# Latent attention: own query tiles summed by GpSimd, four absorbed weight tiles in place of six, and a new order around the shifts

## The chip, the cores and the metric

One core of a Trainium2 chip runs the whole kernel, one launch. The metric is the device time of that launch in microseconds (us), lower is better. The kernel before took 834.43 us (median of three runs, 832.11 to 836.56).

## The reference

The kernel computes a two-layer decoder on 4 x 256 tokens of 256 features. Only the layer-0 cross attention (latent attention with rotary positions) is touched here. Cut to what matters:

```python
q_hk  = (hidden_q @ Wq.T).reshape(B, S, H, K)          # H = 16 heads, K = 128
q_big = einsum('bshk,hkq->bshq', q_hk, w_kc_q)         # 192 latent features per head
q_big = q_big * cos + rotate_half(q_big) * sin         # halves of 96 features change places
kv_r  = kv_c * cos_k + rotate_half(kv_c) * sin_k       # 64 features, shared by all heads
q_r   = einsum('bshq,hqr->bhsr', q_big, W_qr)          # R = 64
k_r   = einsum('bld,hdr->bhlr', kv_r, W_kr)
p     = softmax(einsum('bhsr,bhlr->bhsl', q_r, k_r))
# the values are projected with w_kc_kv and Wo and added to x
```

## The kernel before, in words

`mla_stage` works on eight **pairs** of heads (`PAIRS = 8`), p = 0 to 7. There is no planner: each engine has its own program, written out by hand in queue order, and engines meet only in semaphores, so an instruction that waits holds up everything behind it on its engine. 1024 token columns are handled in two halves of 512 (one PSUM bank each).

Per pair, the query weights of both heads are **folded** (`fold`, L1474: `wq2` x `wkq`, 2 x 192 latent columns side by side). ScalarE copies the high part, VectorE writes the rest (`fold_rest`, L1216). The 384 latent columns make three tiles of 128: tile 0 belongs to head 0, tile 2 to head 1 (the **own** tiles), tile 1 holds 64 columns of each head (the **shared** tile). `packed(p, k)` (L1518, six one-pass matmuls each) projects one tile of one half into a PSUM bank, k = 0 to 5 in the order shared, own 0, own 2 for half 0, then half 1.

`rotate(p, k)` (VectorE) multiplies each bank by the cosine and by the sine table `tab` and writes both products to `qcs`: four 64-row instructions for the shared tile (L1201), two 128-row instructions for an own tile (L1208). The rotary swap of halves isn't done on the queries. Instead the absorbed weights exist twice: `turn` transposes `W_qr` and the key weight, `turned_weights` (ScalarE, L1359 to L1368) lays out six tiles in `wrT`, a plain and a swapped order, `absorb` (L1496) makes six 64-column products with `wkrT`, and `absorbed_weights` (VectorE, L1221) copies them (384 columns). A tile's cosine product meets the plain weights and its sine product the swapped ones, both accumulated in PSUM: `scored_shared` (L1532, two matmuls) and `scored_own` (L1539, four matmuls, each two passes).

The resulting queries leave PSUM as a high part (`query_high`, ScalarE, L1378, two 64-row copies per half) and a rest (`query_rest`, VectorE, L1226). `scores(p, k)`, k = 0 to 7 (L1557), gives scores of one sequence and head. `maximum` (VectorE, L1233) and `denominators` (ScalarE, L1389, two exponentials with sums) follow, then per half `logarithms` (L1394), `shifts` (VectorE, L1239 to L1247), `shift_transpose` (PE, L1567), and `shift_rows` (ScalarE, L1398), which issues two 4 KB DMAs (L1401) that place the shifts as two extra rows of `q2`. `scores_t` (L1595, L1596) needs those rows. It gives transposed, shifted scores, `exponentials` (L1409) makes probabilities, `product` (L1612) the contexts, `context_high` and `context_rest` (L1415, L1256) split them, `project` (L1626) multiplies by the output weight and `add` (L1263) adds to x.

The PE order of one pair is:

```python
project(p-1,0) packed(p,2) turn(p+1) project(p-1,1) packed(p,3) scored_shared(p,0)
project(p-1,2) packed(p,4) output_weight(p) scored_own(p,0) project(p-1,3) packed(p,5)
fold(p+1) scored_shared(p,1) scores(p,0..3) scored_own(p,1) absorb(p+1)
shift_transpose(p,0) scores(p,4..7) scores_t(p,0..1) packed(p+1,0) packed(p+1,1)
shift_transpose(p,1) product(p,0..1) scores_t(p,2..3) product(p,2..3)
```

The VectorE order is: add 0, rotate 2, add 1, rotate 3, add 2, rotate 4, weight_rest, add 3, query_rest twice, rotate 5, fold_rest, maximum 0 to 3, shifts(0), query_rest twice, absorbed_weights, maximum 4 to 7, shifts(1), rotate(p+1, 0 and 1), context_rest 0 to 3. GpSimd has, once per pair and after the first two scores_t, nine instructions (L1185, L1187, L1189) that round the weights of the feed-forward layer. SP issues the weight loads of the next pairs and the copies of the queries to `q2` (L1132).

Of the kernel before, what the change touches and what calls it, by code (L numbers as in the profile page):

```python
# [1007 lines left out]
class PairWeights:  # L1008


    def __init__(self, c, st):
# [7 lines left out]
        self.tab = sb("tab", [P, 2, 3, SEQ])  # L1019
# [15 lines left out]
    def first(self, sp):  # L1035
        self.load_a(sp, 0)
        self.load_k(sp, 0)
        self.load_n(sp, 0)
        sp.dma_start(self.tab[:, :, :, :], self.io["rope_q"]).then_inc(self.tab_in.sem, 16)


def mla_stage(c):
    nc, io = c.nc, c.io
    with ExitStack() as st:
# [9 lines left out]
        wrT, wkrT = sb("wrT", [P, 6, P]), sb("wkrT", [P, 2 * CTX])  # L1054
        wr = sb("wr", [P, 2, 2, 3, R])
# [25 lines left out]
        zeroed, tern = c.counter("at_m5"), c.counter("at_m4")  # L1081
# [40 lines left out]
        def seq_cols(b):  # L1122
            return slice(b * SEQ, (b + 1) * SEQ)

        with nc.Block() as block:

            @block.sync
            def _(sp):
# [18 lines left out]
                for p in range(PAIRS):  # L1147
# [46 lines left out]
            def _(dve):  # L1194
                def rotate(p, k):
# [23 lines left out]
                def absorbed_weights(p, bank):  # L1219
                    dve.wait_ge(absorbed.sem, p + 1)  # L1220
                    dve.tensor_scalar(wr[:, p % 2, :, :, :].rearrange("p j t n -> p (j t n)"),  # L1221
                                      c.ps[:, bank, 0:6 * R], 1.0, None, ALU.mult).then_inc(wr_done.sem, 1)
# [83 lines left out]
                dve.wait_ge(tab_in.sem, 16)  # L1306
# [5 lines left out]
                for p in range(PAIRS):  # L1312
# [37 lines left out]
            def _(act):  # L1350
# [4 lines left out]
                def turned_weights(p):  # L1355
# [3 lines left out]
                    act.activation(dst.rearrange("p (k n) -> p k n", n=DCQ)[:, 0:4:3, :],  # L1359
                                   ps[:, 0:2 * DCQ].rearrange("p (h n) -> p h n", h=2), ACT.Copy)\  # L1360
                        .then_inc(turned_ev.sem, 1)
                    act.activation(dst[:, DCQ:DCQ + 448].rearrange("p (h n) -> p h n", h=2)[:, :, 0:160],
                                   ps[:, 32:352].rearrange("p (h n) -> p h n", h=2), ACT.Copy).then_inc(turned_ev.sem, 1)
                    act.activation(dst[:, 352:416].rearrange("p (h n) -> p h n", h=2),
                                   ps[:, 0:2 * DCQ].rearrange("p (k n) -> p k n", n=32)[:, 0:12:11, :], ACT.Copy)\
                        .then_inc(turned_ev.sem, 1)
# [29 lines left out]
                def shift_rows(p, half):  # L1396
# [68 lines left out]
            def _(pe):  # L1465
                def fold(p):
# [22 lines left out]
                def absorb(p, bank):  # L1489
# [3 lines left out]
                    for j in range(2):  # L1493
                        for tile in range(3):
                            h = (0, j, 1)[tile]
                            mm = pe.matmul(c.ps[:, bank, (3 * j + tile) * R:(3 * j + tile + 1) * R],  # L1496
                                           wrT[:, WR_SLOTS[tile][j], :], wkrT[:, rows(h)],
                                           start=True, stop=True)
# [24 lines left out]
                def scored_shared(p, half):  # L1523
# [1715 lines left out]
```

## Time and profile before

| what | value |
|---|---|
| median of three runs | 834.43 us (832.11 to 836.56) |
| the profiled execution | 833.54 us, span 831.7 us |
| mean granted TensorE clock | 0.948 |
| this stage, from its first matmul to its last add | 113.7 to 425.3 us of the span |
| seven pairs (p = 1 to 7) | start 37.4 us apart |

The span runs from the first to the last instruction that the profile shows, and the run's own time holds 1.8 us around it. Times of single instructions below come from this one execution. PE is the matmul engine, DVE is VectorE, ACT ScalarE, POOL GpSimd, SP the queue that issues DMAs. An fp32 matmul shows as two PE instructions, one declared fp32r as one.

### The profile page before, as it was taken

What the parts mean: (1) busy time and instruction counts of PE and PEld (TensorE: products, weight loads), DVE (VectorE), ACT (ScalarE), POOL (GpSimd) and SP (SyncE); (2) the same over time, 40 slices, a digit from 0 to 9 for tenths busy, and PEclk for the clock granted to TensorE, in tenths of its full rate; (3) what the DMA queues carried; (4) which work ended last, traced back from release to release, by engine and by line L of the source; (5) the groups of instructions that cost most, each with busy time, mean ns of one, the idle gap of its engine ahead of it and who ended that gap; (6) DMA issues with size and microseconds to landing.
All of it is one profiled execution on the core that took longest, in us unless ns stands there. A gap on an engine that the chain in (4) does not pass through costs nothing. (4 is left out here: it accounts for less than half of the span.)

```text
span 831.7 us, 13300 instructions
## 1 busy us (share of the span) xinstructions
PE 720.5 (87%) x4814; PEld 462.6 (56%) x4826; DVE 576.9 (69%) x1109; ACT 430.5 (52%) x896; POOL 198.4 (24%) x298
## 2 busy tenths in 40 slices
PE   5999979999998989999847469999379999759998
PEld 3555656666665656666533345566234444348886
DVE  5678568676667657676569955565578999575666
ACT  4558734544636364543649655555256767433332
POOL 2413010303123030303135314220121111351350
PEclk9999999999999999999989779999869999958999
DMA  4624422120202111110144006220010333303111
GB/s 123 184 82 138 139 67 67 47 56 21 74 10 67 29 48 29 48 42 1 26 119 86 9 12 186 64 55 2 23 36 21 83 71 83 105 2 103 51 51 51
DMA packets 49760, 52.24 MB, mean 63 GB/s; under 512 B 10116, under 2 KB 40388, under 8 KB 49588
## 3 DMA queue, kind: packets, MB, share of 16 engines
q1 hardware_dynamic: 48982, 51.03, 22.6%
q8 instruction: 39, 0.64, 0.3%
q10 hardware_dynamic: 714, 0.37, 0.2%
q14 instruction: 25, 0.20, 0.1%
HBM read 26.58 MB, written 2.04 MB: 34 GB/s over the span
## 5 line engine op out<-in xcount | busy, mean ns | idle before, releaser
L427 DVE TENSOR_REDUCE a_nm<-ps 128x2 f32<-128x512 f32 (+1 forms) x112 | 75.4, 688 | 28.2 <-PE ps L723 18.1
L2480 DVE TENSOR_REDUCE x_nm<-ps 128x2 f32<-128x512 f32 x128 | 85.0, 687 | 13.0 <-PE ps L2621 10.8
L2565 ACT ACTIVATE x_pt<-ps 128x1024 f32<-128x1024 f32 x64 | 62.5, 1021 | 33.9 <-PE ps L2649 33.2
L1389 ACT ACTIVATE m_junk<-ps,m_nm 128x256 bf16<-128x256 f32 x128 | 58.7, 486 | 30.3 <-DVE m_nm L1233 30.3
L1518 PE MATMUL ps<-m_xp,m_mp 128*128 128x512 f32 x288 | 73.4, 395 | 1.0 <-DVE m_wr L1221 1.0
L1185 POOL TENSOR_SCALAR fw<-fw,finv 128x256 f32<-128x256 f32 x24 | 11.6, 485 | 232.8 <-PE ps L1596 232.8
L2621 PE MATMUL ps<-kx,a_qs 96*128 96x256 bf16 x256 | 52.3, 291 | 8.5 <-DMA a_qs<-a_ks 6.5
L1518 PEld LDWEIGHTS ps<-m_xp,m_mp 128*128 128x128 f32 x288 | 51.3, 188 | 13.1 <-issue 3.2
L3049 PE MATMUL ps<-x_xp,x_wp 128*128 128x512 f32 x216 | 55.1, 406 | 0.0
L1201 DVE TENSOR_TENSOR m_qcs<-ps,mw_tab 64x512 f32<-64x512 f32 x64 | 44.1, 689 | 7.6 <-PE ps L1518 4.3
L3049 PEld LDWEIGHTS ps<-x_xp,x_wp 128*128 128x128 f32 x216 | 41.2, 196 | 8.5
L1208 DVE TENSOR_TENSOR m_qcs<-ps,mw_tab 128x512 f32<-128x512 f32 x64 | 41.2, 685 | 5.4 <-PE ps L1518 4.9
L2665 PE MATMUL ps<-x_pt,a_ks 128*32 128x256 f32 x512 | 42.0, 400 | 2.6 <-DVE x_av L2489 2.6
L2621 PEld LDWEIGHTS ps<-kx,a_qs 96*128 96x128 bf16 x256 | 20.2, 101 | 41.9 <-issue 13.1
L1233 DVE TENSOR_REDUCE m_nm<-ps 128x2 f32<-128x512 f32 x64 | 40.2, 682 | 0.9 <-PE ps L1557 0.7
L2649 PE MATMUL ps<-a_qs,kx 98*128 98x512 bf16 x128 | 39.4, 391 | 0.0
L1557 PE MATMUL ps<-m_kHH,m_qs 128*128 128x256 f32 x128 | 34.7, 306 | 4.4 <-DVE m_qs L1226 4.2
L1409 ACT ACTIVATE m_pt<-ps 128x1024 f32<-128x1024 f32 x32 | 31.1, 1019 | 13.8 <-PE ps L1596 13.8
L575 ACT ACTIVATE a_pt<-ps 128x1024 f32<-128x1024 f32 x32 | 32.1, 1020 | 10.4 <-PE ps L758 10.4
L575 ACT ACTIVATE fw<-ps 128x1024 f32<-128x1024 f32 (+1 forms) x32 | 25.8, 810 | 21.9 <-PE ps L774 15.1
L1256 DVE TENSOR_TENSOR m_cp<-ps,m_cp 128x256 fp32r<-128x256 f32 x32 | 12.8, 420 | 34.0 <-ACT m_cp L1415 34.0
L1595 PE MATMUL ps<-m_qs,m_kHH 128*128 128x512 f32 x64 | 27.6, 431 | 9.8 <-issue 9.5
(305 smaller groups left out, 1692.2 us busy)
## 6 DMA issues: line engine op xcount, KB each, us to landing
a_qs<-a_parts SPq DMA_DIRECT2D x48, 128.0 KB
a_ks<-a_parts SPq DMA_DIRECT2D x48, 128.0 KB
m_q<-m_qs SPq DMA_DIRECT2D x32, 128.0 KB
x_gb<-scr_g SPq DMA_DIRECT2D x8, 512.0 KB, 3.7
fw<-in_f_w SPq DMA_DIRECT2D x12, 256.0 KB
a_qs<-a_ks SPq DMA_DIRECT2D x48, 64.0 KB
mw_wq<-in_m_wq SPq DMA_DIRECT2D x8, 256.0 KB, 2.9
mw_wo<-in_m_wo SPq DMA_DIRECT2D x8, 256.0 KB, 2.8
```

Source lines behind the costliest of these rows:

```text
L427: dve.tensor_reduce(dst, src, AX.X, ALU.max, negate=True).then_inc(mx_done.sem, 1)
L575: act.activation(pt[:, n % 2, kt, 0:banks * BANK], c.ps[:, 2 + 2 * kt:2 + 2 * kt + banks, :].rearrange("p b n -> p (b n)"), ACT.Exp, scale ...
L1201: dve.tensor_tensor(qcs[rows((cs, 1 - cs)[h]), half, 1, h, :].rearrange("p (b q) -> p b q", q=SEQ), c.ps[rows(h), QB_BANKS[k], :].rearrang ...
L1208: dve.tensor_tensor(qcs[:, half, tile, cs, :].rearrange("p (b q) -> p b q", q=SEQ), c.ps[:, QB_BANKS[k], :].rearrange("p (b q) -> p b q", ...
L1233: dve.tensor_reduce(nm[:, k // 4, first:first + QT], c.ps[:, S_BANKS[k % 4], :].rearrange("p (t k) -> p t k", t=QT), AX.X, ALU.max, negate ...
L1389: act.activation(junk[:, n % 4, :], c.ps[:, S_BANKS[k % 4], qt * SEQ:(qt + 1) * SEQ], ACT.Exp, bias=nm[:, k // 4, one], accum_out=den[:, k ...
L1518: mm = pe.matmul(c.ps[:, QB_BANKS[k], :], mp[:, p % 2, w, dt, tile * P:(tile + 1) * P], xp[:, x, dt, half_cols(half)], start=((dt, w, x) = ...
L2480: dve.tensor_reduce(nm[:, n % ITEMS, QT * u:QT * u + QT], c.ps[:, u % 2, :].rearrange("p (t k) -> p t k", t=QT), AX.X, ALU.max, negate=Tru ...
L2565: act.activation(pt[:, n % 2, kt, :], c.ps[:, 2 + 2 * kt:4 + 2 * kt, :].rearrange("p b n -> p (b n)"), ACT.Exp, scale=SCALE).then_inc(exp_ ...
L2621: mm = pe.matmul(c.ps[:, u % 2, qt * SEQ:(qt + 1) * SEQ], queries(slice(0, S_ROWS), n, u).squeeze(1)[:, qt * P:(qt + 1) * P], kx[0:S_ROWS, ...
L2665: mm = pe.matmul(c.ps[rows(h), 6, 0:SEQ], vs[:, QT * b + kt, g, :], pt[:, n % 2, kt, h * SEQ:(h + 1) * SEQ], start=(kt == 0), stop=(kt == ...
L3049: mm = pe.matmul(up_bank(j, half), wp[:, b, w, at:at + EH], xp[:, x, dt, cols(half)], start=((dt, w, x) == terms[0]), stop=((dt, w, x) == ...
```

## The change

The latent columns of each head are placed in another order: the own tile of a head now holds the first 64 columns of each of its two rotary halves (0 to 63 and 96 to 159), the shared tile the other 32 of each half. With that the rotary partner of a row of an own tile is 64 rows away in the same tile. `rotate` writes the sine product of an own tile already swapped (two 64-row instructions) and the cosine product as before (one of 128 rows), and GpSimd adds the two in `qcs`. So own tiles need the plain weights only: four weight tiles in `wrT` and `wr`, two matmuls in `scored_own`. `fold` writes its columns in two pieces each. VectorE makes the high part of the first head's queries in the second half and its rest before `shifts(p, 0)`, and PE puts `scores(p, 4)` before `shift_transpose(p, 0)`. SP issues one of the two shift DMAs of the first half. `packed(p+1, 1)` moves behind `product(p, 1)`, `rotate(p+1, 1)` behind two `context_rest`. The table load becomes seven DMAs.

```diff
-        self.tab = sb("tab", [P, 2, 3, SEQ])
+        self.tab = sb("tab", [P, 2, 2, SEQ])
-        sp.dma_start(self.tab[:, :, :, :], self.io["rope_q"]).then_inc(self.tab_in.sem, 16)
+        for tile, (to, rows, source) in (...seven pieces...):
+            sp.dma_start(self.tab[to:to + rows, :, tile, :], self.io["rope_q"][first:first + rows, :, k, :])\
+                .then_inc(self.tab_in.sem, 16)
@@ sync, end of each pair
                     copy_queries(p, 1)
+                    sp.wait_ge(mt.sem, 2 * p + 1)
+                    send_shifts(sp, 0, 1)
@@ gpsimd
+                def own_tile(p, half, h):
+                    pool.wait_ge(rope.sem, rotated(p, 3 * half + 2 + h))
+                    turned_part = qcs[:, half, OWN_TILES[h], 1, :]
+                    plain = qcs[:, half, OWN_TILES[h], 0, :]
+                    pool.tensor_tensor(plain, plain, turned_part, ALU.add).then_inc(whole.sem, 1)
+
+                own_tile(0, 0, 0)
                 for p in range(PAIRS):
+                    own_tile(p, 0, 1)
+                    own_tile(p, 1, 0)
+                    own_tile(p, 1, 1)
+                    if p + 1 < PAIRS:
+                        own_tile(p + 1, 0, 0)
                     pool.wait_ge(stt.sem, 4 * p + 2)
@@ vector: rotate, own tile
-                    for cs in range(2):
+                    for part in range(2):
                         dve.tensor_tensor(
-                            qcs[:, half, tile, cs, :].rearrange("p (b q) -> p b q", q=SEQ),
-                            c.ps[:, QB_BANKS[k], :].rearrange("p (b q) -> p b q", q=SEQ),
-                            tab[:, cs, tile, :].unsqueeze(1).broadcast_to([P, 2, SEQ]), ALU.mult)\
+                            qcs[rows(1 - part), half, tile, 1, :].rearrange("p (b q) -> p b q", q=SEQ),
+                            c.ps[rows(part), QB_BANKS[k], :].rearrange("p (b q) -> p b q", q=SEQ),
+                            tab[rows(part), 1, 0, :].unsqueeze(1).broadcast_to([R, 2, SEQ]), ALU.mult)\
                             .then_inc(rope.sem, 1)
+                    dve.tensor_tensor(
+                        qcs[:, half, tile, 0, :].rearrange("p (b q) -> p b q", q=SEQ),
+                        c.ps[:, QB_BANKS[k], :].rearrange("p (b q) -> p b q", q=SEQ),
+                        tab[:, 0, 0, :].unsqueeze(1).broadcast_to([P, 2, SEQ]), ALU.mult)\
+                        .then_inc(rope.sem, 1)
@@ vector: absorbed_weights, and a new query_high
-                                      c.ps[:, bank, 0:6 * R], 1.0, None, ALU.mult).then_inc(wr_done.sem, 1)
+                                      c.ps[:, bank, 0:4 * R], 1.0, None, ALU.mult).then_inc(wr_done.sem, 1)
+                def query_high(p):
+                    dve.wait_ge(qr.sem, 2 * p + 2)
+                    dve.tensor_scalar(qs[rows(0), 0, half_cols(1)], c.ps[rows(0), 5, :], 1.0, None, ALU.mult)\
+                        .then_inc(q_hi.sem, 1)
@@ vector: order
                         maximum(p, k)
+                    query_high(p)
+                    query_rest(p, 1, 0)
                     shifts(p, 0)
-                    query_rest(p, 1, 0)
                     query_rest(p, 1, 1)
                         rotate(p + 1, 0)
+                    context_rest(p, 0)
+                    context_rest(p, 1)
+                    if p + 1 < PAIRS:
                         rotate(p + 1, 1)
-                    for b in range(BATCH):
-                        context_rest(p, b)
+                    context_rest(p, 2)
+                    context_rest(p, 3)
@@ scalar: turned_weights (three copies of 384, 320 and 64 columns become four of 256, 128, 64 and 64)
@@ scalar: query_high, shift_rows
-                    for h in range(2):
+                    if half:
+                        act.wait_ge(q_hi.sem, 4 * p + 3)
+                    for h in range(half, 2):
-                    for h in range(2):
-                        act.dma_start(...)
+                    send_shifts(act, half, 0)
+                    if half:
+                        send_shifts(act, half, 1)
@@ tensor: fold, absorb, scored_own
-                            mm = pe.matmul(c.ps[:, 6 + dt, h * DCQ:(h + 1) * DCQ], wq2[:, h, dt * P:(dt + 1) * P],
-                                           wkq[:, h, :], start=True, stop=True)
+                            by_half = wkq[:, h, :].rearrange("p (s n) -> p s n", s=2)
+                            own, shared = ((0, P), (P, DCQ)) if h == 0 else ((DCQ + R, 2 * DCQ), (DCQ, DCQ + R))
+                            for (a, b), part in ((own, by_half[:, :, 0:OWN]), (shared, by_half[:, :, OWN:])):
+                                mm = pe.matmul(c.ps[:, 6 + dt, a:b], wq2[:, h, dt * P:(dt + 1) * P], part,
+                                               start=True, stop=True)
-                    for j in range(2):
-                        for tile in range(3):
+                    for slot in range(4):
-                    pe.wait_ge(rope.sem, rotated(p, 3 * half + 3))
-                    for cs in range(2):
-                        for h, tile in ((0, 0), (1, 2)):
+                    pe.wait_ge(whole.sem, whole.at(4 * p + 2 * half + 2))
+                    for h in range(2):
@@ tensor: order
+                    scores(p, 4)
                     shift_transpose(p, 0)
-                    for k in range(4, 8):
+                    for k in range(5, 8):
                         packed(p + 1, 0)
-                        packed(p + 1, 1)
                     shift_transpose(p, 1)
                     product(p, 0)
                     product(p, 1)
+                        packed(p + 1, 1)
```

## Rows read from the trace of the kernel before

**Rows 1.** The page: span, busy time of each engine.

```profile
PE 720.5 (87%) x4814; PEld 462.6 (56%) x4826; DVE 576.9 (69%) x1109; ACT 430.5 (52%) x896; POOL 198.4 (24%) x298
```

**Rows 2.** Busy time by stretch: us, then each engine's, PEclk, DMA share, GB/s.

```profile
198.70:236.10 37.40, 34.61 (x196) 23.07 (x195) 25.31 (x45) 18.40 (x55) 7.21 (x9) 1.00 0.15 43
...
370.40:373.80 3.40, 3.21 (x15) 3.24 (x16) 2.96 (x6) 1.37 (x6) 0.00 (x0) 0.50 0.35 80
```

**Rows 3.** Timeline of PE, pair 3: start, us, what, idle before and releaser.

```profile
236.09 0.98 PE L1626 MATMUL ps<-m_wn,m_cp 128*128 128x256 f32 x6
...
244.99 1.89 PE L1539 MATMUL ps<-m_qcs,m_wr 128*64 128x512 f32 x8
...
249.01 1.46 PE L1474 MATMUL ps<-mw_wkq,mw_wq 128*128 128x192 f32 x8
...
255.31 1.55 PE L1496 MATMUL ps<-m_wkrT,m_wrT 128*128 128x64 f32 x12
257.61 0.28 PE L1567 MATMUL ps<-ident,m_m 128*16 128x128 f32 x1 [0.74 <-DVE m_m L1247]
258.41 0.36 PE L1557 MATMUL ps<-m_kHH,m_qs 128*128 128x256 f32 x1 [0.53 <-DVE m_qs L1226]
...
263.23 2.96 PE L1518 MATMUL ps<-m_xp,m_mp 128*128 128x512 f32 x12
...
266.23 1.95 PE L1612 MATMUL ps<-m_pt,m_kvr 128*64 128x256 f32 x16
...
269.18 0.47 PE L1595 MATMUL ps<-m_qs,m_kHH 128*128 128x512 f32 x1 [1.00 <-issue]
...
273.49 0.98 PE L1626 MATMUL ps<-m_wn,m_cp 128*128 128x256 f32 x6
```

**Rows 4.** Timeline of DVE, pair 3.

```profile
241.31 2.85 DVE L1201 TENSOR_TENSOR m_qcs<-ps,mw_tab 64x512 f32<-64x512 f32 x4 [0.69 <-PE ps L1518]
...
244.80 1.28 DVE L1208 TENSOR_TENSOR m_qcs<-ps,mw_tab 128x512 f32<-128x512 f32 x2
...
247.82 0.69 DVE L1263 TENSOR_TENSOR x<-ps,x 128x512 f32<-128x512 f32 x1 [1.41 <-PE ps L1626]
...
252.22 2.48 DVE L1233 TENSOR_REDUCE m_nm<-ps 128x2 f32<-128x512 f32 x4
256.98 0.17 DVE L1239 TENSOR_TENSOR m_md<-m_nm,m_lnd 128x8 f32<-128x8 f32 x1 [2.28 <-ACT m_lnd L1394]
...
259.50 2.48 DVE L1233 TENSOR_REDUCE m_nm<-ps 128x2 f32<-128x512 f32 x4
```

**Rows 5.** Timeline of ACT, pair 3.

```profile
256.85 1.19 ACT L1378 ACTIVATE m_qs<-ps 64x512 fp32r<-64x512 f32 x2
...
264.12 1.92 ACT L1409 ACTIVATE m_pt<-ps 128x1024 f32<-128x1024 f32 x2
266.33 0.27 ACT L1398 ACTIVATE m_mT<-ps 16x128 fp32r<-16x128 f32 x1 [0.29 <-PE ps L1567]
266.63 1.30 ACTq L1401 DMA_DIRECT2D m_q<-m_mT  x2
```

**Rows 6.** SP: the query copies of pair 3's second half, and the table load.

```profile
257.45 1.11 SPq L1132 DMA_DIRECT2D m_q<-m_qs  x2
...
L1039 SPq DMA_DIRECT2D mw_tab<-in_rope_q x1: 433/433/433, 96.2 to 96.2; - x1
```

**Rows 7.** POOL additions by line: ns min/median/max, first and last start us.

```profile
L1178 POOL TENSOR_TENSOR m_kvr<-m_qcs x1: 1307/1307/1307, 124.4 to 124.4; 128x512 f32<-128x512 f32 x1
...
L1865 POOL TENSOR_TENSOR f_h<-f_h,fw x7: 2346/2367/3252, 446.0 to 462.5; 128x1024 f32<-128x1024 f32 x7
```

**Rows 8.** Pair 0: busy time of 125.8 to 142.7 us, and DVE's first maxima.

```profile
125.80:142.70 16.90, 16.90 (x90) 10.47 (x88) 16.54 (x25) 6.42 (x18) 0.00 (x0) 1.00 0.34 82
...
140.21 2.47 DVE L1233 TENSOR_REDUCE m_nm<-ps 128x2 f32<-128x512 f32 x4
```

**Rows 9.** Timeline of PE: the first projection of pair 7's start.

```profile
386.03 0.98 PE L1626 MATMUL ps<-m_wn,m_cp 128*128 128x256 f32 x6
```

More of the change, by code:

```diff
@@ L1038, in first @@
         self.load_n(sp, 0)
-        sp.dma_start(self.tab[:, :, :, :], self.io["rope_q"]).then_inc(self.tab_in.sem, 16)
+        for tile, (to, rows, source) in ((0, (0, 64, (0, 0))), (0, (64, 32, (0, 96))), (0, (96, 32, (1, 0))),
+                                         (1, (0, 32, (0, 64))), (1, (32, 32, (1, 32))),
+                                         (1, (64, 32, (0, 64))), (1, (96, 32, (1, 32)))):
+            k, first = source
+            sp.dma_start(self.tab[to:to + rows, :, tile, :], self.io["rope_q"][first:first + rows, :, k, :])\
+                .then_inc(self.tab_in.sem, 16)
 def mla_stage(c):
@@ L1123, in seq_cols, with send_shifts @@
             return slice(b * SEQ, (b + 1) * SEQ)
+        def send_shifts(queue, half, h):
+            queue.dma_start(q2[R:R + 2, h, half_cols(half)].bitcast(F32),
+                            mT[NM * h:NM * h + NM, half, :].bitcast(F32)).then_inc(m_in[half].sem, 16)
         with nc.Block() as block:
@@ L1358, in turned_weights @@
                     dst = wrT[:, :, :].rearrange("p t n -> p (t n)")
[L1359 to L1366, printed above, removed]
+                    turned_in = ps[:, 0:2 * DCQ].rearrange("p (h s n) -> p h s n", h=2, s=2)
+                    act.activation(dst.rearrange("p (k s n) -> p k s n", k=4, s=2)[:, 0:4:3, :, :],
+                                   turned_in[:, :, :, 0:OWN], ACT.Copy).then_inc(turned_ev.sem, 1)
+                    act.activation(dst[:, P:P + 2 * DCQ].rearrange("p (h n) -> p h n", h=2)[:, :, 0:R]
+                                   .rearrange("p h (s n) -> p h s n", s=2),
+                                   turned_in[:, :, :, OWN:], ACT.Copy).then_inc(turned_ev.sem, 1)
+                    swapped = dst[:, DCQ:DCQ + P].rearrange("p (h s n) -> p h s n", h=2, s=2)
+                    for k in range(2):
+                        act.activation(swapped[:, :, 1 - k, :], turned_in[:, :, k, OWN:], ACT.Copy)\
+                            .then_inc(turned_ev.sem, 1)
                     for h in range(2):
@@ L1492, in absorb @@
                         pe.wait_ge(mp_lo.sem, p + 1)
-                    for j in range(2):
-                        for tile in range(3):
[L1495 to L1498, printed above, removed]
+                    for slot in range(4):
+                        mm = pe.matmul(c.ps[:, bank, slot * R:(slot + 1) * R], wrT[:, slot, :], wkrT[:, rows(slot // 2)],
+                                       start=True, stop=True)
                     mm.then_inc(absorbed.sem, 1)
@@ L1531, in scored_shared @@
                     for h in range(2):
-                        pe.matmul(c.ps[rows(h), 4 + half, :], wr[:, p % 2, h, 1, :], qcs[:, half, 1, h, :],
+                        pe.matmul(c.ps[rows(h), 4 + half, :], wr[:, p % 2, SHARED_SLOTS[h], :], qcs[:, half, 1, h, :],
                                   start=True, stop=False, skip_group_check=True)
                 def scored_own(p, half):
-                    pe.wait_ge(rope.sem, rotated(p, 3 * half + 3))
-                    for cs in range(2):
-                        for h, tile in ((0, 0), (1, 2)):
-                            mm = pe.matmul(c.ps[rows(h), 4 + half, :], wr[:, p % 2, cs, tile, :],
-                                           qcs[:, half, tile, cs, :], start=False, stop=(cs == 1),
-                                           skip_group_check=True)
+                    pe.wait_ge(whole.sem, whole.at(4 * p + 2 * half + 2))
+                    for h in range(2):
+                        mm = pe.matmul(c.ps[rows(h), 4 + half, :], wr[:, p % 2, OWN_SLOTS[h], :],
+                                       qcs[:, half, OWN_TILES[h], 0, :], start=False, stop=True,
+                                       skip_group_check=True)
                     mm.then_inc(qr.sem, 1)
@@ L1702, in mla_stage @@
                      (dn, 16 * PAIRS), (ln_done, 2 * PAIRS), (ms, 6 * PAIRS), (wn_lo, PAIRS), (tern, 9 * PAIRS),
-                     (zeroed, 2)):
+                     (zeroed, 2), (whole, 4 * PAIRS)):
             s.done(n)
```

21 lines of the change are left out of this document (11 added, 10 removed).

## The prediction

> **What bounds the kernel now.** I read the page first: PE is busy 87% of the span, DVE 69% [rows 1]. That is an average over stages, so I took the busy time by pair. A middle pair lasts 37.40 us, PE is busy 34.6 of them, DVE 25.3, ACT 18.4, POOL 7.2, at full clock [rows 2]. This looks like a stage bound by PE. The timelines say it less simply. Times below count from the start of a pair's first projection, 236.09 in pair 3 [rows 3].
>
> PE has no gap up to 20.7. There it waits for the shifts (0.74), then for a query rest (0.53), and before the third scores_t for "issue" (1.00), which is the second shift DMA [rows 3]: issued at 266.63, 1.30 us for both, and 1.25 more to 269.18 [rows 3, 5]. DVE works with one wait of 1.41 from 241.31 until after its first maxima (254.70), and waits 2.28 for the logarithm [rows 4]. So behind PE there is a **ring** of waits, which I write as segments:
>
> - a, 0 to rotate 4: 8.71
> - b, rotate 4 to maximum 0: 7.42
> - c, maximum 0 to shifts(0), eight exponentials with sums on ACT: 4.76
> - d, shifts(0) to maximum 4: 2.52
> - e, maximum 4 to the first exponentials: 4.62
> - f, these to the shift rows: 2.21
> - g, shift rows to the next pair's start: DMA, two scores_t, two products: 7.16
>
> They sum to 37.40 [rows 3 to 5]. What the change is worth must be read off this ring, with PE as the check.
>
> **What changes on PE.** scored_own has 8 instructions of 0.23 (1.89 less its tail) and keeps 4: 0.9 less, twice. absorb has 12 at 0.12 and keeps 8: 0.5 less [rows 3]. fold gets 16 in place of 8. No row shows its new shapes. The lower bound is absorb's pace for 64 columns, 2.0 in place of 1.4. The upper one is fold's own 0.17 for 192 columns, 2.8 [rows 3]. I take 2.0, since pieces of 64 and 128 columns are nearer to absorb's. Net 1.7 less per pair (0.9 at the other bound).
>
> **What changes on DVE.** Four 64-row instructions take 2.85, so one starts every 0.72. An own tile's two take 1.29 [rows 4]. Three take 0.72 + 0.72 + 0.69 = 2.13: 0.84 more for each of four own tiles. absorbed_weights copies 256 columns in place of 384: 0.13 less by 0.69/512 a column, some of it fixed.
>
> **The ring after.**
>
> - a: rotate 2 gets longer inside idle time (rotate 3 still starts when its bank does, at 5.2). A 64-row instruction starts 0.72 after the one before it, a 128-row one 0.60 (1.28 less 0.68): +0.12 ahead of rotate 4.
> - b: +0.84 for rotate 4 and +0.84 for rotate 5. The wait of 1.41 [rows 4] goes, because project 3 comes 0.9 earlier and DVE later, and with it 0.2 of smaller gaps: 7.47, +0.05. Before, fold's start was 3.21 ahead of maximum 0 [rows 3, 4]. Fold now starts at 12.0 and takes 0.6 more, so its rest could be done for 15.8 against the 16.3 at which maximum 0 comes. At the upper bound, 16.6: +0.3 per pair.
> - c: unchanged. The new query_high and one query_rest on DVE (0.72 each, by the 64-row row) lie in the 2.28 that it waits for the logarithm and end 0.8 before it [rows 4]. Were that cover gone, they'd cost 1.44. The rest frees scores(p, 4), 0.6 on PE, which also ends before the shifts are there.
> - d: one query_rest fewer behind the shifts (-0.72), and -0.13 for the copy: 1.67. ACT's remaining copy of 0.6 [rows 5] starts at the logarithm's end as before, in time.
> - e: unchanged. scores 5 to 7 start 0.6 earlier.
> - f: shift rows waited 0.29 for a transpose that stood behind both packed [rows 5]. Now only packed(p+1, 0) stands ahead of it: 1.95, -0.26.
> - g: unchanged. product 1 waits for the shift rows (0.3), then takes 1.0, and packed(p+1, 1) 1.4 [rows 3]: it ends 2.7 after their start, the DMA lands 2.85 after. A cover of only 0.15; half a packed more would show.
>
> Sum: +0.12 + 0.05 - 0.85 - 0.26 = **-0.94** in pairs 1 to 6.
>
> **Moved DMAs and queues.** SP now waits for the shift rows of the first half. Ahead of it stand the two query copies (1.11 [rows 6]), done 0.2 before. Behind it stand the weight loads of the pair after, issued from 258.6 on and first used after 273.49, some 15 us later. With one DMA on each queue the first half's rows land 0.65 sooner, which only keeps pace with scores 5 to 7. Seven table DMAs at 0.43 each [rows 6] are 3 us of SP at 96 us, 29 before the first rotation: nothing. POOL has four additions per pair of 1.31 [rows 7] beside the rounding of 7.2. The addition for pair p+1 stands ahead of the rounding, so that starts at about 35.7 and ends at 6.5 of the next pair, the next addition at 7.9. scored_own wants it at 8.9 (244.99 [rows 3]): slack 1.0. In the second half rotate 5 ends at 15.5, its sum is there at 16.9, and PE comes at 17.1 (absorb's 255.31 less the 1.9 of scored_own is 17.35; less 0.9, more 0.6). Behind it PE has slack anyway.
>
> **Pairs 0 and 7.** In pair 0 DVE is busy 16.54 of 16.90 up to its last first-half maximum [rows 8], so the four longer rotations go in whole: maximum 0, now at 140.21, comes 3.4 later. From there the pair gains 0.85 + 0.26: +2.3. Pair 7 has no turn, so rotate 2 is longer ahead of rotate 3 too: 0.6 + 0.12 + 2 x 0.84 - 1.41 = +1.0, then -0.72 in d and nothing in f, as no packed is there to move: +0.3. No row shows it, and I allow 1 either way.
>
> **Clock.** From 370.4 to 373.8 the granted clock is 0.50, the 1.2 GHz level [rows 2], after PE had idled at the shifts. Pair 6 lost 0.34 by it: pair 7 starts at 386.03, and 236.09 + 4 x 37.40 is 385.69 [rows 3, 9]. In pair 2 it stayed at 1.00 [rows 2]. The change takes work from exactly this place (absorb, scored_own), so I expect it there in most pairs, at 0.1 each, since the scores now have slack: +0.7.
>
> **Sum:** 2.3 - 6 x 0.94 + 0.3 + 0.7 = -2.3. On the profiled execution (833.54) that is 831.2; the median of before lies 0.9 above it, so 832.1.
>
> **Rivals.**
>
> *A, PE is the bound.* Then each of seven pairs gives the 1.7 of PE, -12, about 822.5, and up to 826 with fold at its upper bound. For it: 93% busy. Against: DVE has no gap to absorb 1.7 more in segment b. 0.2.
>
> *B, the clock takes it back.* In each pair PE runs at 0.50 through scores and scores_t. At pair 6's price that is 7 x 0.34 = 2.4 on top of 2.3 - 5.6 + 0.3 = -3.0: 833.8. If packed and shift_transpose(1) get late too, the 0.94 is gone and +2.6 is left: 837. I put it at 835.5. For it: pair 6 [rows 2, 9]; against: the full clock of a pair with the same two idle places [rows 2]. 0.15. The Trainium skill (TensorE: Matmul & The Clock Gate, Part 1) says that the low clock is the default and activity releases it, which would make B more likely than that pair does.
>
> *C, slower: POOL is late for scored_own(p, 0).* The decisive point is the slack of 1.0. One POOL addition of seven took 3252 ns where the least took 2346 [rows 7]. At that ratio, 1.39, rounding and additions end at 11.6, scored_own is 2.7 late, fold starts at 14.7, and maximum 0 comes at 18.5: +2.2 per pair, net +1.3 for six, with pair 0's part about +10: 844. Against: POOL's 7.21 is the same in the pair with a different DVE load beside it. 0.15. The Trainium skill (SBUF — State Buffer, Who interferes with whom) says that a GpSimd instruction that reads SBUF and a VectorE one with two SBUF inputs shut each other out. Here only the tiny shift instructions are of that kind, the rotations read PSUM and one table, so by that rule C stays out.
>
> **How the numbers follow.** Forecast 0.5, with its own range 828.5 to 836. My measurement can tell about 0.5% (4.2 us). Of the forecast's 0.5, 0.14 falls over 0.5% faster (rotations overlapping better than 0.72), 0.03 slower. A is faster (0.2), B 0.13 same and 0.02 slower, C 0.01 same and 0.14 slower. So faster 0.34, same 0.47, slower 0.19. The range 824.5 to 839 leaves out C and the lower part of A, 0.2 together.
>
> **What would show it.** Right: pairs 36.4 to 36.6 apart; own tiles 2.1 on DVE; no wait of DVE before add 3; maximum 0 in pair 0 at 143.6; PE idle before the shift transpose over 1 us in two parts; fold near 2.0; POOL's additions near 1.3 with the last well before scored_own. Wrong: PE waiting for POOL ahead of scored_own(p, 0) (C), pairs near 35.7 (A), or a clock at 0.50 in a pair's packed and product as well (B).

## The result, and the profile after

The changed kernel is **slower**: median 839.41 us (five runs, 838.85 to 840.88) against 834.41 for the kernel before in the same session (831.12 to 836.56). The ratio over all these runs is 1.0078, 95% interval 1.0049 to 1.0107 (the two medians alone would give 1.0060; the ratios below are of the first kind). The forecast was 832.1, the range 824.5 to 839.0, so the time lies just outside it, on the side that got a chance of 0.19.

The page of the kernel after, its busy times and the clock in 40 slices (compare [rows 1]):

```profile
span 837.2 us, 13322 instructions
PE 722.6 (86%) x4782; PEld 474.9 (57%) x4794; DVE 605.8 (72%) x1149; ACT 427.5 (51%) x896; POOL 239.0 (29%) x330
PEclk9999999899898989899988779999869999958999
```

The stage lies in slices 6 to 21. Before, all of them but the last showed 9. Five of those now show 8 as well (slices 8, 11, 13, 15 and 17); the 8 of slice 21 both kernels have. PE has 32 matmuls fewer and is busy 2.1 us longer. Where it goes can be seen when the middle pair, pair 3, is cut where the clock changes. Columns: stretch, its length, busy time of PE, PEld, DVE, ACT and POOL, granted clock, DMA share, GB/s (compare the pair of [rows 2]):

```profile
239.38:260.90 21.52, 19.78 (x116) 13.89 (x116) 18.65 (x31) 8.36 (x29) 10.59 (x12) 0.99 0.13 34
260.90:267.20 6.30, 5.74 (x20) 4.89 (x21) 4.09 (x9) 4.72 (x20) 0.00 (x0) 0.50 0.43 133
267.20:276.90 9.70, 9.51 (x57) 6.05 (x55) 6.28 (x12) 4.91 (x8) 1.73 (x2) 0.99 0.00 1
```

The clock is 0.50, the 1.2 GHz level, for **6.3 us**, and so it is in every pair from 0 to 6, for 6.3 to 6.6 us. Before, that happened in pair 6 alone of these, for 3.4 us [rows 2]. Pair 7 has some 3.4 us of it in both kernels. The timeline of PE in pair 3 of after: start, us, instruction, and in brackets the idle time before it and what released it (compare [rows 3]):

```profile
239.38 0.97 PE L1669 MATMUL ps<-m_wn,m_cp 128*128 128x256 f32 x6
...
248.26 1.03 PE L1582 MATMUL ps<-m_qcs,m_wr 128*64 128x512 f32 x4
...
251.41 1.95 PE L1521 MATMUL ps<-mw_wkq,mw_wq 128*128 128x128 f32 x16
...
257.35 1.10 PE L1541 MATMUL ps<-m_wkrT,m_wrT 128*128 128x64 f32 x8
259.56 0.36 PE L1600 MATMUL ps<-m_kHH,m_qs 128*128 128x256 f32 x1 [1.11 <-DVE m_qs L1262]
...
261.02 0.38 PE L1610 MATMUL ps<-ident,m_m 128*16 128x128 f32 x1 [0.74 <-DVE m_m L1283]
261.85 0.55 PE L1600 MATMUL ps<-m_kHH,m_qs 128*128 128x256 f32 x1 [0.45 <-DVE m_qs L1262]
262.20 0.42 PE L1600 MATMUL ps<-m_kLL,m_qs 128*128 128x256 f32 x1
...
264.55 0.63 PE L1638 MATMUL ps<-m_qs,m_kHH 128*128 128x512 f32 x1
...
269.09 0.27 PE L1610 MATMUL ps<-ident,m_m 128*16 128x128 f32 x1
269.29 1.95 PE L1655 MATMUL ps<-m_pt,m_kvr 128*64 128x256 f32 x16
271.16 1.66 PE L1562 MATMUL ps<-m_xp,m_mp 128*128 128x512 f32 x6
...
276.90 0.98 PE L1669 MATMUL ps<-m_wn,m_cp 128*128 128x256 f32 x6
```

PE now idles three times with little between: 1.11 ahead of scores(p, 4), 0.74 ahead of the shift transpose, 0.45 ahead of scores(p, 5). That is 2.3 us where the kernel before had 0.74 and 0.53 [rows 3]. From there on a scores matmul shows 0.41 in place of 0.28, a scores_t 0.63 in place of 0.40. DVE and ACT of the same pair (compare [rows 4, 5]):

```profile
249.63 0.69 DVE L1239 TENSOR_TENSOR m_qcs<-ps,mw_tab 128x512 f32<-128x512 f32 x1
...
250.57 0.68 DVE L1299 TENSOR_TENSOR x<-ps,x 128x512 f32<-128x512 f32 x1
...
255.63 2.48 DVE L1269 TENSOR_REDUCE m_nm<-ps 128x2 f32<-128x512 f32 x4
...
260.39 0.17 DVE L1275 TENSOR_TENSOR m_md<-m_nm,m_lnd 128x8 f32<-128x8 f32 x1 [0.97 <-ACT m_lnd L1438]
...
262.07 0.68 DVE L1269 TENSOR_REDUCE m_nm<-ps 128x2 f32<-128x512 f32 x1
263.08 0.69 DVE L1269 TENSOR_REDUCE m_nm<-ps 128x2 f32<-128x512 f32 x1 [0.32 <-PE ps L1600]
```

```profile
266.80 2.13 ACT L1453 ACTIVATE m_pt<-ps 128x1024 f32<-128x1024 f32 x2
269.39 0.27 ACT L1442 ACTIVATE m_mT<-ps 16x128 fp32r<-16x128 f32 x1 [0.46 <-PE ps L1610]
```

The ring can be read off these, from 239.38. Maximum 0 comes at 16.25 (forecast 8.83 + 7.47 = 16.30), and add 3 (250.57) has no wait. The shifts follow after 4.76, maximum 4 after 1.68. Up to there the pair is as forecast. Then maximum 4 to the exponentials takes 4.73, these to the shift rows 2.59 (forecast 1.95), and the rest 7.51 (forecast 7.16). These three segments lie in and behind the slow stretch.

The span account, after less before. Stage start is the first m_stats instruction (113.69 and 113.27). The pair starts are the projections' (161.41 and 164.41 for pair 1, 386.03 and 389.53 for pair 7), the end of the stage the next norm's first instruction (425.83 and 429.77):

| part | before | after | difference | forecast |
|---|---|---|---|---|
| up to the stage | 113.69 | 113.27 | -0.42 | 0 |
| pair 0 | 47.72 | 51.14 | +3.42 | +2.3 |
| pairs 1 to 6 | 224.62 | 225.12 | +0.50 | -5.6 |
| pair 7 | 39.80 | 40.24 | +0.44 | +0.3 |
| rest of the program | 405.87 | 407.43 | +1.56 | 0 |
| span | 831.7 | 837.2 | +5.5 | -2.3 (with +0.7 for the clock) |

The rest of the program is the same code in both. Its 1.56 is taken up behind the experiments.

### The profile page after: what moved, and what is told of

It is laid out like the page before. It is cut to its first block and busy times, and to the rows that moved or that the text cites. A ratio compares the mean times of both kernels' runs of the same rounds, so it can differ in the third digit from the quotient of the medians.

```text
span 837.2 us, 13322 instructions
## 1 busy us (share of the span) xinstructions
PE 722.6 (86%) x4782; PEld 474.9 (57%) x4794; DVE 605.8 (72%) x1149; ACT 427.5 (51%) x896; POOL 239.0 (29%) x330
## 5 line engine op out<-in xcount | busy, mean ns | idle before, releaser
L1198 POOL TENSOR_TENSOR m_qcs<-m_qcs 128x512 f32<-128x512 f32 x32 | 41.2, 1286 | 186.1 <-DVE m_qcs L1239 186.1
L2525 DVE TENSOR_REDUCE x_nm<-ps 128x2 f32<-128x512 f32 x128 | 84.8, 686 | 11.3 <-PE ps L2666 9.0
L1562 PE MATMUL ps<-m_xp,m_mp 128*128 128x512 f32 x288 | 75.2, 397 | 0.9 <-DVE m_wr L1252 0.9
L1227 DVE TENSOR_TENSOR m_qcs<-ps,mw_tab 64x512 f32<-64x512 f32 x64 | 44.1, 689 | 16.1 <-PE ps L1562 12.3
L1600 PE MATMUL ps<-m_kHH,m_qs 128*128 128x256 f32 x128 | 42.1, 352 | 14.4 <-DVE m_qs L1262 13.0
L1234 DVE TENSOR_TENSOR m_qcs<-ps,mw_tab 64x512 f32<-64x512 f32 x64 | 44.1, 689 | 6.7 <-PE ps L1562 4.9
L1269 DVE TENSOR_REDUCE m_nm<-ps 128x2 f32<-128x512 f32 x64 | 41.9, 686 | 5.5 <-PE ps L1600 5.5
L1600 PEld LDWEIGHTS ps<-m_kHH,m_qs 128*128 128x128 f32 x128 | 30.5, 239 | 24.9 <-ACT m_junk L1433 11.0
L1600 PE MATMUL ps<-m_kLL,m_qs 128*128 128x256 f32 x128 | 39.3, 330 | 0.0
```

The lines of the kernel that those rows point to most:

```text
L1227: dve.tensor_tensor(qcs[rows((cs, 1 - cs)[h]), half, 1, h, :].rearrange("p (b q) -> p b q", q=SEQ), c.ps[rows(h), QB_BANKS[k], :].rearrang ...
L1234: dve.tensor_tensor(qcs[rows(1 - part), half, tile, 1, :].rearrange("p (b q) -> p b q", q=SEQ), c.ps[rows(part), QB_BANKS[k], :].rearrange ...
L1269: dve.tensor_reduce(nm[:, k // 4, first:first + QT], c.ps[:, S_BANKS[k % 4], :].rearrange("p (t k) -> p t k", t=QT), AX.X, ALU.max, negate ...
L1562: mm = pe.matmul(c.ps[:, QB_BANKS[k], :], mp[:, p % 2, w, dt, tile * P:(tile + 1) * P], xp[:, x, dt, half_cols(half)], start=((dt, w, x) = ...
L1600: mm = pe.matmul(c.ps[:, S_BANKS[k % 4], qt * SEQ:(qt + 1) * SEQ], qs[:, h, q0:q0 + P], part[:, seq_cols(b)], start=(low == 0), stop=(low ...
L2525: dve.tensor_reduce(nm[:, n % ITEMS, QT * u:QT * u + QT], c.ps[:, u % 2, :].rearrange("p (t k) -> p t k", t=QT), AX.X, ALU.max, negate=Tru ...
```

## The experiments

Theory for all: the time lost is the clock, and what takes the clock is that PE idles ahead of and between scores(p, 4), the transpose and scores(p, 5). Its rivals: the longer VectorE path costs it, GpSimd does, or the removed PE work matters for itself. Below, "per pair" is the mean distance of the starts of pairs 1 to 7, from each kernel's profile.

### Filling the idle places with matmuls that nobody reads

e1_fill is the kernel after with eight matmuls more per pair, into PSUM bank 7, which nothing reads at that time:

```diff
+                def fill(p, n):
+                    if p + 1 < PAIRS:
+                        for _ in range(n):
+                            pe.matmul(c.ps[:, 7, :], kHH[:, 0:P], kLL[:, 0:BANK], start=True, stop=True)
@@ tensor, order
                         absorb(p + 1, 6)
+                    fill(p, 4)
                     scores(p, 4)
+                    fill(p, 3)
                     shift_transpose(p, 0)
+                    fill(p, 1)
```

> The changed kernel plus matmuls that compute nothing of use (into a free PSUM bank, first seven pairs): four behind absorb, three behind scores(p, 4), one behind shift_transpose(p, 0), at 0.23 us each, so that TensorE doesn't idle there. Theory (the lowered clock in each pair takes the gain back): granted clock 1.00 through the pair, pairs 36.5 apart in place of 37.5, about 832 us, 7 below the changed kernel. Rival (the longer rotations or POOL set the pair, the clock is a bystander): pairs stay at 37.5 or grow by what the fillers overshoot, 839.5 or more, even at full clock.

Measured: **827.39 us** (before 833.72), ratio 0.9941, interval 0.9919 to 0.9963. 56 matmuls more make the kernel 12 us faster than after, 11.3 when each is held against the kernel before of its own session (-6.33 and +5.00). I had expected 7. By the two profiles 3.7 of the 12 lie behind the stage, in code that is the same. Per pair 36.25. Its PE timeline in pair 3, and the busy times of the stretch:

```profile
235.83 0.98 PE L1669 MATMUL ps<-m_wn,m_cp 128*128 128x256 f32 x6
...
254.73 1.18 PE L1687 MATMUL ps<-m_kLL,m_kHH 128*128 128x512 f32 x4
...
256.56 0.86 PE L1687 MATMUL ps<-m_kLL,m_kHH 128*128 128x512 f32 x3
...
258.29 0.36 PE L1600 MATMUL ps<-m_kHH,m_qs 128*128 128x256 f32 x1 [0.31 <-DVE m_qs L1262]
...
272.08 0.98 PE L1669 MATMUL ps<-m_wn,m_cp 128*128 128x256 f32 x6
```

```profile
255.00:264.00 9.00, 8.14 (x40) 5.49 (x39) 5.48 (x15) 7.37 (x29) 0.00 (x0) 1.00 0.39 107
```

The clock stays at 1.00, and the segments are what was forecast. Maximum 0 (DVE), the maxima of the second half, the exponentials and the shift rows (ACT):

```profile
252.09 2.47 DVE L1269 TENSOR_REDUCE m_nm<-ps 128x2 f32<-128x512 f32 x4
...
258.52 2.47 DVE L1269 TENSOR_REDUCE m_nm<-ps 128x2 f32<-128x512 f32 x4
```

```profile
263.13 1.92 ACT L1453 ACTIVATE m_pt<-ps 128x1024 f32<-128x1024 f32 x2
264.94 0.25 ACT L1442 ACTIVATE m_mT<-ps 16x128 fp32r<-16x128 f32 x1
```

16.26, then 6.43 (forecast 4.76 + 1.67), 4.61, 1.81 and 7.14: 36.25. After's 37.52 is 1.27 more: 0.12 up to the exponentials (DVE waits 0.32, 0.16 and 0.16 for scores, and its last maximum starts 2.72 behind the first where e1 takes some 1.8; but ACT needs 0.9 for the two exponentials behind each maximum and is the slower of the two in both, so little of it comes through), 0.78 to the shift rows (longer exponentials, then the transpose that stands behind a late packed) and 0.37 behind them.

That last piece is the thin cover of the prediction. In e1 the two products start 0.75 ahead of the shift rows (264.19), in after 0.10 (269.29). packed(p+1, 1) stands behind them, so in after the third scores_t starts 3.27 behind the shift rows (272.66 less 269.39), where e1 needs 2.91 (267.85 less 264.94).

### Each half of the change alone

e2_own_only is the kernel after with all orders put back: own tiles on GpSimd, no moves. e3_moves_only is the kernel before with the moves alone:

```diff
 # e3: added to before, e2: taken out of after
                         maximum(p, k)
+                    query_high(p)
+                    query_rest(p, 1, 0)
                     shifts(p, 0)
-                    query_rest(p, 1, 0)
@@ tensor
+                    scores(p, 4)
                     shift_transpose(p, 0)
-                    for k in range(4, 8):
+                    for k in range(5, 8):
@@ tensor, behind product(p, 1)
+                        packed(p + 1, 1)
@@ sync
+                    sp.wait_ge(mt.sem, 2 * p + 1)
+                    send_shifts(sp, 0, 1)
```

> The changed kernel with all moves undone: own tiles summed by GpSimd, four weight tiles, but the order of before (no early query of VectorE, scores(p, 4) behind the transpose, both packed together, both shift DMAs on ACT). Theory: with 1.35 us of PE work gone from the place where PE waits for the shifts, the clock falls there in most pairs, and without the moves nothing is won: pair 0 costs 3.4, each pair 0.1 plus 0.5 to 1.5 for the clock, so 841 to 848. Rival (the moves are what costs, the sum on GpSimd is neutral): 834 to 838.

> The kernel before plus the moves alone (early high part and rest of one query on VectorE, scores(p, 4) ahead of the transpose, one shift DMA on SP, packed(p+1, 1) behind product 1, rotate(p+1, 1) behind two context rests), with the old rotations and six weight tiles. Theory: 0.72 in segment d and 0.26 in segment f per pair, no cost in pair 0; the clock stays up because scored_own and absorb keep their length: pairs 36.4 apart, about 827.5. If the clock falls all the same, 832 to 835. Rival (the moves themselves cost): over 835.

e2: **845.71**, ratio 1.0142 (1.0119 to 1.0164), 38.08 per pair, as expected. e3: **824.42**, ratio 0.9891 (0.9871 to 0.9912), 36.28 per pair, 3 us better than expected. So the moves carry the gain and the own tiles the loss. Against the kernel before of the session (833.72) the moves gain 9.3 without the own tiles. With them they gain 7.0: e2 is 12.0 above its before, after 5.0 above its own. PE and the clock of e3, pair 3, whose pair starts at 234.35:

```profile
253.55 1.55 PE L1513 MATMUL ps<-m_wkrT,m_wrT 128*128 128x64 f32 x12
255.21 0.35 PE L1574 MATMUL ps<-m_kHH,m_qs 128*128 128x256 f32 x1
...
255.84 0.28 PE L1584 MATMUL ps<-ident,m_m 128*16 128x128 f32 x1
256.67 0.36 PE L1574 MATMUL ps<-m_kHH,m_qs 128*128 128x256 f32 x1 [0.55 <-DVE m_qs L1237]
```

```profile
234.00:270.00 36.00, 34.66 (x194) 22.85 (x192) 25.93 (x46) 17.67 (x54) 7.21 (x9) 1.00 0.16 44
```

With the longer absorb and scored_own still there, PE reaches scores(p, 4) when its queries are ready. Around the transpose it idles 0.55 in all, and the clock is 1.00 in pairs 1 to 6. In e2 it idles 2.50 and 0.53, and the clock falls:

```profile
263.84 0.28 PE L1596 MATMUL ps<-ident,m_m 128*16 128x128 f32 x1 [2.50 <-DVE m_m L1276]
264.65 0.55 PE L1586 MATMUL ps<-m_kHH,m_qs 128*128 128x256 f32 x1 [0.53 <-DVE m_qs L1255]
```

```profile
264.50:267.90 3.40, 3.25 (x15) 3.28 (x16) 2.82 (x5) 1.37 (x7) 0.00 (x0) 0.51 0.63 164
```

### Moves, with the last gaps filled

e4_moves_fill is e3 with 2, 3 and 1 of e1's matmuls at the same three places.

> As the moves alone, plus fillers (two behind absorb, three behind scores(p, 4), one behind shift_transpose(p, 0)). If the moves alone already run at full clock: the same time within 1 us. If their clock falls: full clock here and about 827.5. Rival (fillers cost what they take): 1 to 3 us over the moves alone.

Measured: 823.95, ratio 0.9891 (0.9869 to 0.9912), 36.50 per pair. No difference to e3 that can be measured. There was no clock to win back in pairs 1 to 6, and the fillers overran by 0.2 a pair. Pair 0 is 0.95 shorter in e4 (46.65 against 47.60), but not by the fillers. In e3's profile the clock is 0.51 from 119.2 to 126.1, in e4's it is 1.00 there, and e4's first filler starts only at 144.29. The projections in that place, e3 and then e4:

```profile
123.53 4.15 PE L1535 MATMUL ps<-m_xp,m_mp 128*128 128x512 f32 x12 [0.42 <-DVE m_wr L1227]
...
122.95 2.97 PE L1535 MATMUL ps<-m_xp,m_mp 128*128 128x512 f32 x12 [0.98 <-DVE m_wr L1227]
```

Why the clock was low around there in e3 (and in e5, e7 and e8) and not in the other kernels, no run shows.

### Only the PE work away

e5_less_pe is the kernel before with the lighter PE work of the change and the narrower copy of VectorE that goes with it, nothing else. scored_own omits the sine products of the own tiles, absorb makes four tiles in place of six, and scored_shared uses the first head's shared tile for both heads. So the queries lack a part, and e5 and e6 serve for timing only. e6_less_pe_fill adds 7 filler matmuls behind absorb and 2 behind the transpose.

```diff
 # absorb, scored_own, absorbed_weights
-                        for tile in range(3):
+                        for tile in range(3 - 2 * j):
-                    for cs in range(2):
+                    for cs in range(1):
-                                      c.ps[:, bank, 0:6 * R], 1.0, None, ALU.mult).then_inc(wr_done.sem, 1)
+                                      c.ps[:, bank, 0:4 * R], 1.0, None, ALU.mult).then_inc(wr_done.sem, 1)
```

> The kernel before with nothing but PE work taken out: two of the four matmuls of each scored_own, two of the six of absorb (and 128 columns of their copy). It leaves out the sine part of the own tiles, so the queries aren't the reference's. VectorE's rotations, GpSimd and the order are those of before. Theory (idle PE ahead of the shift transpose lowers the clock, and the scores then run at half rate on the path): slower than before although it does strictly less, pairs near 37.9, 836 to 842. Rival (PE work is what the pair costs, or idle time costs nothing): 1.35 to 1.8 us less per pair, 820 to 825, or no change.

> The same with less PE work, plus seven filling matmuls behind absorb and two behind shift_transpose(p, 0) in the first seven pairs. Theory: clock 1.00, pairs 37.3 (the 0.13 of the shorter copy), 832 to 834: the removed PE work was worth nothing in time, since the ring doesn't run through it. Rival (PE-bound): 1 us or more per pair faster than before, under 827.

Both **missed** on the level. Only the sign of their difference held. e5: 830.64 (before 832.99), ratio 0.9966 (0.9953 to 0.998), 37.01 per pair. e6: 827.04, ratio 0.9913 (0.9892 to 0.9935), 36.38 per pair. The clock falls in e5 in pair 0 and in pairs 2 to 6 (not in pair 1, where PE idles as long), and the fillers give 0.63 per pair back. In pair 3 of e5:

```profile
257.70:261.20 3.50, 3.50 (x17) 3.31 (x16) 2.82 (x6) 2.29 (x10) 0.00 (x0) 0.52 0.75 210
```

What I had overlooked is the other wait. The scored_own(p, 0) of before stands ahead of project 3, and add 3 waits for that [rows 4]. With 0.9 less ahead of it, DVE's wait of 1.41 is 0.55 in e5:

```profile
246.66 0.69 DVE L1263 TENSOR_TENSOR x<-ps,x 128x512 f32<-128x512 f32 x1 [0.55 <-PE ps L1626]
```

So that part of PE's work is on the ring. All that e6 leaves out is worth 37.44 - 36.38 = 1.06 per pair at full clock, 0.86 of it by this wait. The full change gives it back: the own tiles' two longer rotations in the same segment take 2 x 0.84.

### The own tiles at full clock, and a control

e7_own_fill is e2 with 8 fillers behind absorb and 2 behind the transpose. e8_before_fill is the kernel before with 3 and 2, which checks whether fillers help by themselves.

> The own-tile part alone (order of before) plus eight filling matmuls behind absorb and two behind the transpose. Theory: at full clock the ring gives 37.40 + 0.12 + 0.05 - 0.13, so pairs near 37.4, and pair 0 costs 3.4: 836 to 838, some 8 below the own-tile part without fillers (845.7). Rival (GpSimd's sums or the longer rotations cost beyond pair 0): pairs over 37.7 at clock 1.00, over 839.

> Control: the kernel before plus three filling matmuls behind absorb and two behind shift_transpose(p, 0). Theory: pairs stay at 37.40, pair 6 loses its 0.3 of lowered clock: the time of before within 1 us. Rival (fillers win or cost by themselves, so that the other filled runs can't be read as clock): more than 2 us either way.

e7: 836.86, ratio 1.0044 (1.0028 to 1.0059), 37.36 per pair, 0.72 less than e2. e8: 832.73, ratio 0.9989 (0.9973 to 1.0004), 37.37 per pair. Fillers alone do nothing where the clock already holds. The own tiles at full clock are worth nothing per pair (37.36 against 37.44), and cost 3.6 in pair 0 (51.31 against 47.72) and 1.3 in pair 7 (41.12 against 39.80). Part of this is clock: in e7's pair 0 it is 0.50 from 121.7 to 128.3, in before it isn't. Without such a stretch, e1 against e4, pair 0 costs 3.3 (49.97 less 46.65). The moves on top of them give 37.36 - 36.25 = 1.11 per pair.

### Which of the gaps

e9_fill_early is e1 with the 4 fillers behind absorb alone, e10_fill_late e1 with only the 3 and 1 behind scores(p, 4) and behind the transpose.

> The changed kernel with only the four filling matmuls behind absorb (0.93 us of the 1.1 that PE waits for the early query), nothing in the 0.74 and 0.45 behind. Theory: what is left idle is less than in the kernel before (0.74 and 0.53), whose clock held in six pairs of seven, so the clock holds here in most pairs too: pairs 36.3 and 827 to 829. If it falls all the same: 37.0 to 37.5, 832 to 839.

> The changed kernel with only the later fillers (three behind scores(p, 4), one behind the transpose), so that the 1.1 us behind absorb stay idle. Theory: 1.1 idle in one piece is less than the 1.27 of the kernel before, but the stretch ahead of it is thinner by the 1.35 us of scored_own and absorb that are gone; I expect the clock to hold in most pairs, 827 to 831. If only the total of PE work ahead counts, it falls in some pairs: 831 to 836.

e9: 827.34, ratio 0.9925 (0.9908 to 0.9942). e10: 827.66, ratio 0.9929 (0.9911 to 0.9948). Both are as expected. Either place gives the time back. In e10 the clock held in all of pairs 1 to 6. In e9 it fell in two of the six, and those lasted 36.6 in place of 36.2. One of them, pair 2, whose PE idles 0.74 and 0.55 as in the four pairs that kept the clock:

```profile
200.00:236.00 36.00, 34.40 (x194) 24.28 (x193) 28.54 (x50) 17.38 (x55) 11.67 (x13) 0.95 0.16 44
```

### The account of all kernels

All from one profile each (that of e2 is its slowest run, 847.43). The stage runs from its first statistics to the next norm's. The kernel before had medians of 832.99 to 834.41 in the four sessions.

| kernel | median us | pair 0 | per pair, 1 to 6 | pair 7 | stage | rest |
|---|---|---|---|---|---|---|
| before | 834.41 | 47.72 | 37.44 | 39.80 | 312.14 | 405.9 |
| after | 839.41 | 51.14 | 37.52 | 40.24 | 316.50 | 407.4 |
| e1_fill | 827.39 | 49.97 | 36.25 | 39.78 | 307.26 | 403.8 |
| e2_own_only | 845.71 | 52.66 | 38.08 | 41.07 | 322.23 | 409.6 |
| e3_moves_only | 824.42 | 47.60 | 36.28 | 39.30 | 304.57 | 405.0 |
| e4_moves_fill | 823.95 | 46.65 | 36.50 | 39.24 | 304.86 | 403.2 |
| e5_less_pe | 830.64 | 49.33 | 37.01 | 39.38 | 310.78 | 405.0 |
| e6_less_pe_fill | 827.04 | 47.60 | 36.38 | 39.47 | 305.37 | 406.6 |
| e7_own_fill | 836.86 | 51.31 | 37.36 | 41.12 | 316.60 | 405.5 |
| e8_before_fill | 832.73 | 48.58 | 37.37 | 39.79 | 312.59 | 403.8 |
| e9_fill_early | 827.34 | 49.98 | 36.38 | 39.78 | 308.02 | 403.6 |
| e10_fill_late | 827.66 | 50.03 | 36.29 | 40.26 | 308.02 | 403.8 |

The rest of the program is the same code in all and lasts between 403.2 and 409.6. It holds 1.6 us of after against before, and 3.7 of the 12 between after and e1, which the stage doesn't explain. A part can be read: ACT's first instruction of the rest, behind which the square root of the norm stands, waits for a DMA that is issued as the stage ends (425.78 before, 429.72 after, 420.58 in e1) and lands 3.6, 4.8 and 3.1 us later. Before, then after:

```profile
429.41 1.13 ACT L2184 ACTIVATE kx_ordered<-kx_raw 128x512 f32<-128x512 f32 x1 [8.10 <-DMA kx_raw<-in_ctx]
...
434.57 1.12 ACT L2229 ACTIVATE kx_ordered<-kx_raw 128x512 f32<-128x512 f32 x1 [9.31 <-DMA kx_raw<-in_ctx]
```

That is 1.2 of the 1.6, and 1.7 of the 3.7. The clock isn't it: the mean of the rest is 0.90 before and after. Why the same DMA takes longer, and where the other differences come from, was not tried and stays **open**. The stage alone gives e1 9.2 us on after.

Both e3 and e4 are faster than both kernels. The version to ship is the moves alone: 824.42, 1.1% under before.

## Why the prediction was wrong

**The failed step is "Clock"**: "I expect it there in most pairs, at 0.1 each, since the scores now have slack: +0.7." The place and the frequency were right, in all pairs in fact, and the price was wrong by more than a factor of ten: 1.27 per pair in 1 to 6 (37.52 against e1's 36.25), and 1.2 in pair 0 (51.14 against 49.97). Six times the one and the other once are 8.8 us. Put in the place of the 0.7, they turn -2.3 into +5.8. Less the 1.3 by which the ring itself came out better (below) that is +4.5, and the stage moved +4.4 (316.50 less 312.14). Two things made the term small:

- It took pair 6's 3.4 us at 0.50 [rows 2] as the size of an event. Here each lasts 6.3 us, over the transpose, scores 5 to 7 and the first two scores_t. The kernel before shows no event of that length in this stage.
- It gave the scores slack and looked no further. They had some: only 0.12 of the 1.27 falls there. The scores_t and the packed ahead of the second transpose, and with them the exponentials, had none (0.78), nor had the products (0.37).

**Rival B** was the mechanism, with its signs (the clock in each pair, the 0.94 gone), at 0.15 and priced at 835.5, from pair 6 again. Its worse branch (837) asked that packed and the second transpose be late. They are, by 0.46 of ACT's wait. The chance was held down because pair 2 kept the full clock "with the same two idle places". But the change makes three places with 2.3 us of them where before had 1.27. The prediction knew of more idle time (its signs of being right name over 1 us ahead of the transpose, in two parts) and didn't use it for the clock. The Trainium skill (TensorE: Matmul & The Clock Gate, Part 1) says that the low clock is the default and that activity releases it. By that rule B was the likelier, and after and e1 agree with it: 0.50 where PE idles, 1.00 where matmuls that nobody reads fill the same time.

**The ring held.** Point by point, against e1 or after:

- fold: forecast 2.0, measured 1.95. Own tiles: forecast 2.13 on DVE, measured 2.10 (1.41 and 0.69, busy). The wait before add 3 is gone.
- a and b: maximum 0 at 16.25 and 16.26 of the pair, forecast 16.30.
- d: 1.68 in after, forecast 1.67. f: 1.81 in e1, forecast 1.95. The moves' terms were 0.72 in d and 0.26 in f, 0.98 in all (the other 0.13 of d is the narrower copy). e3 gives 1.16, of which 0.06 is the lowered clock of before's pair 6, and e1 against e7 gives 1.11. So the moves gave slightly more than forecast.
- Sum: forecast 36.46 per pair, e1 36.25. Sixfold 0.2 is -1.3 us that the forecast left out.
- Pair 0: +2.3 forecast, +2.25 in e1 (49.97 against 47.72), the rest is the clock again. Its maximum 0 was forecast for 143.6 and comes at 143.28:

```profile
143.28 2.48 DVE L1269 TENSOR_REDUCE m_nm<-ps 128x2 f32<-128x512 f32 x4
```

- Pair 7: +0.3 forecast, +0.44 measured, 0.0 in e1.

**Rival A**, PE as the bound, is out. e3 has all of the PE work that e1 dropped, and its pairs take 36.28 against 36.25. But e5 shows that a part of it, 0.9 ahead of project 3, was on the ring, as the prediction's own b has it.

**Rival C**, GpSimd late, is out as well. The additions of after by line (ns least, median, greatest), and who waited for them:

```profile
L1198 POOL TENSOR_TENSOR m_qcs<-m_qcs x32: 1262/1288/1299, 130.4 to 404.9; 128x512 f32<-128x512 f32 x32
...
  PE ps L1582: 3.4, 4
```

One takes 1.29, forecast 1.31. None of 32 is drawn out, though DVE is at work beside them. PE waits for them in four places, in pairs 0 and 7. In pair 3 the addition is done at 247.89 and scored_own starts at 248.26. The slack is 0.4, not the 1.0 of the forecast, so C's point of decision was closer than it looked. The Trainium skill (SBUF — State Buffer, Who interferes with whom) says that a VectorE instruction with two SBUF inputs contends with a GpSimd one that reads SBUF. VectorE's rotations, additions and rests in this stage have one such input, and the 1262 to 1299 ns agree with the rule. The longest of those four waits is 1.98, in pair 0 (C as a whole was priced at about 10 us):

```profile
135.03 1.08 PE L1582 MATMUL ps<-m_qcs,m_wr 128*64 128x512 f32 x4 [1.98 <-POOL m_qcs L1198]
```

## What to carry to other kernels

When a change takes work off PE ahead of a wait for another engine, what is taken can become idle time there, and its price can be the clock behind it, as here. Add up the idle places of the new order, compare them with a stretch of the old profile whose clock fell or held, and price every engine's wait behind the stretch at the low clock, not PE's slack alone. A few matmuls into a free PSUM bank are a cheap test of it, and the two halves of a change run apart show which one carries the gain.

## What the hardware showed that was not expected

- Three short idle places, 1.11, 0.74 and 0.45 us, with little work between them, go with 6.3 us at 1.2 GHz in every pair, and this repeats in all of pairs 0 to 6. With 0.55 us idle (e3) it never came in this place. With 0.74 and 0.53 (before) the clock fell in one of pairs 1 to 6, for 3.4 us.
- The idle time alone doesn't decide it. With 1.06 to 1.12 and 0.31, and fillers between them (e10), the clock held in all of pairs 1 to 6. With 0.74 and 0.55 (e9) it fell in two of six, and with 2.05 and 0.53 (e5) in five of six, though the idle places of these pairs are the same to 0.02 us.
- 56 matmuls whose result nobody reads make the kernel 12.0 us faster (839.41 to 827.39, 11.3 against the kernel before of each session), and the same idea on the kernel before makes no difference (832.73 against 832.99).
- Unchanged code behind the stage took 403.2 to 409.6 us in different kernels.
